# Experts: routing weights spread over partitions by DMA through device memory, shared expert as one block, rings of three

## The reference

```python
scores = sigmoid(x @ gate_w.T); choice = scores + e_bias        # 16 experts in 4 groups
# two best groups of four (by the sum of each group's best two), then the four best experts in them
topk_weight = scores[topk] / (sum + 1e-20) * 2.5
g = einsum('th,eih->eti', x, gate_proj); u = einsum('th,eih->eti', x, up_proj)   # 16 experts, 64 inner features
expert_out = einsum('eti,ehi->eth', silu(g) * u, down_proj)
y = einsum('tkh,tk->th', expert_out[topk_idx], topk_weight)
shared_out = silu(x @ shared_gate_w.T) * (x @ shared_up_w.T) @ shared_down_w.T
x = x + y + shared_out
```

## Time and profile before

| | us |
|---|---|
| median of 3 runs | 2615.48 (2614.51 to 2615.79) |
| the profiled execution, its own time | 2611.66 |
| its span, first to last instruction | 2609.8 |
| PE busy in the span | 2134.6 (82%) |
| DVE busy | 2013.6 (77%) |
| ACT busy | 1856.5 (71%) |
| POOL busy | 1645.0 (63%) |
| DMA, mean over the span | 6 GB/s |

### The profile page before, as it was taken

One profiled execution on the slowest core, in us unless ns is written; L12 is line 12 of the kernel. 1 busy time (PEld: TensorE's weight loads), 2 busy tenths in 40 slices (PEclk: granted clock), 3 DMA queues, 4 the chain that ended last, 5 costly groups with the idle time before them and its releaser, 6 DMA issues. The chain is left out here.

```text
span 2609.8 us, 51267 instructions
## 1 busy us (share of the span) xinstructions
PE 2134.6 (82%) x15144; PEld 1559.0 (60%) x15144; DVE 2013.6 (77%) x6071; ACT 1856.5 (71%) x3189; POOL 1645.0 (63%) x1508
## 2 busy tenths in 40 slices
PE   4999999999999789999966667666666776666599
PEld 3777777777777678888844444444444444433367
DVE  4777777777777666776658998999999899999522
ACT  2766666666676533334328999999999999999743
POOL 3667667777677200000028999999999999999600
PEclk7999999999999889999975666676776657767599
DMA  5000000000000000000000000000000000000011
GB/s 136 2 2 2 1 1 0 1 1 0 1 0 2 1 1 1 0 0 0 1 1 1 1 1 0 0 0 0 0 0 0 0 0 0 0 0 1 1 37 36
DMA packets 25280, 14.83 MB, mean 6 GB/s; under 512 B 2952, under 2 KB 24878, under 8 KB 25166
## 3 DMA queue, kind: packets, MB, share of 16 engines
q1 hardware_dynamic: 16846, 9.36, 1.3%
q10 hardware_dynamic: 8320, 4.19, 0.6%
HBM read 9.36 MB, written 4.19 MB: 5 GB/s over the span
## 5 line engine op out<-in xcount | busy, mean ns | idle before, releaser
L1445 POOL TENSOR_TENSOR u<-u,spare 128x1024 f32<-128x1024 f32 x256 | 597.1, 2375 | 41.6 <-ACT spare L1418 41.6
L553 ACT ACTIVATE prob<-s_ps,nmax 128x128 f32<-128x128 f32 (+1 forms) x1024 | 364.4, 432 | 140.2 <-DVE nmax L610 139.9
L1338 PE MATMUL d_ps<-rowsT 28*128 28x256 f32 x1024 | 171.7, 417 | 326.9 <-DVE u L1517 326.4
L610 DVE CUSTOM_DVE_ANT_0 s_ps<-s_ps,mask 128x128 f32<-128x128 f32 (+1 forms) x1024 | 340.7, 385 | 101.4 <-issue 78.0
L1338 PEld LDWEIGHTS d_ps<-rowsT 28*128 28x128 f32 x1024 | 111.6, 253 | 430.2 <-issue 429.5
L1513 DVE TENSOR_SCALAR u<-d_ps 128x1024 f32<-128x1024 f32 x256 | 311.9, 1218 | 41.7 <-PE i_ps L1338 41.1
L590 POOL TENSOR_TENSOR g_lo<-g_all,g_hi 128x512 fp32r<-128x512 f32 x256 | 329.0, 1285 | 21.4
L1517 DVE SCALAR_TENSOR_TENSOR u<-i_ps,u 128x1024 f32<-128x1024 f32 x256 | 313.5, 1225 | 14.8
L1456 POOL TENSOR_TENSOR spare<-spare,u 128x1024 f32<-128x1024 f32 x128 | 303.1, 2368 | 10.7
L1665 POOL MEMSET rows<- 128x4096 f32 x1 | 3.5, 3512 | 427.8 <-POOLq L352 427.8
L1432 ACT ACTIVATE u<-u 128x1024 f32<-128x1024 f32 x256 | 257.8, 1067 | 0.0
(11 more groups left out here) (267 smaller groups left out, 5699.6 us busy)
## 6 DMA issues: line engine op xcount, KB each, us to landing
x<-L_attn_x ACTq DMA_DIRECT2D x8, 512.0 KB, 13.8
y<-y_rows SPq DMA_DIRECT2D x16, 256.0 KB, 2.3
wkqv<-L_attn_Wkqv SPq DMA_DIRECT2D x4, 528.0 KB, 8.6
gate_rows<-L_ffn_gate_proj SPq DMA_DIRECT2D x1, 512.0 KB, 14.5
up_rows<-L_ffn_up_proj SPq DMA_DIRECT2D x1, 512.0 KB, 11.5
down_cols<-L_ffn_down_proj SPq DMA_DIRECT2D x1, 512.0 KB, 12.9
w<-L_ffn_w SPq DMA_DIRECT2D x2, 256.0 KB, 3.0
consts_sb<-consts SPq DMA_DIRECT2D x1, 256.0 KB, 4.4
```

The source lines that it names most:

```text
L553: last = nc.scalar.activation(prob[:, kind, at, :].rearrange("p c n -> p (c n)"), s_ps[kind][:, at.start * P:at.stop * P], ACT.Exp, bias=n ...
L610: last = nc.vector.tensor_tensor_reduce(out=scores, in0=scores, in1=keep.mask[:, N - width:N], scale=-1.0, scalar=3.4e38, op0=ALU.add, op1 ...
L1338: last = nc.tensor.matmul(ps[:, e * W2 + j * N:e * W2 + (j + 1) * N], rowsT[at, slot(i, p), 1, j * P:(j + 1) * P], rowsT[at, slot(i, p), 0 ...
L1445: nc.gpsimd.tensor_tensor(u[:, slot(i, p), :], u[:, slot(i, p), :], spare[:, p % SPARE, :], ALU.add).then_inc(sum_done, 1)
```

## The change

Four things change together in `moe`, and their preparation in `load_and_fold`:

1. The routing weights are no longer split into a high and a low part and spread by a matmul. They are turned (16 rows), copied to `wT`, written by a DMA to `w_rows` in device memory, read back by two DMAs that repeat each expert's row over 64 partitions, and land in `w_all`. VectorE's second product then reads `w_all` in place of `w_ps`.
2. The shared expert's gate and up weights stand side by side in one block of 128 columns, so that its slot has three matmuls instead of six.
3. `g_ps`, `u_ps`, `act_g` and `inter` have three buffers, and the down product follows two slots behind (`LAG`) instead of one.
4. The tables move: `WEIGHTS_AT` is (13, 14) for the two chunks of the next pair, and `ROUTE_AT` is 6 to 12 without a gap.

```diff
-    TAKEN = (0, 5, 11, 16, 17, 19, 23, 28)
+    TAKEN = (0, 5, 11, 16, 17, 19, 23, 26)
-    TURN_AT, LOGITS_AT, WEIGHTS_AT = (1, 3), (2, 4), 6
-    SCORE_AT, SPLIT_AT, ROUTE_AT = 5, (2, 14), (6, 7, 8, 10, 12, 13, 15)
+    TURN_AT, LOGITS_AT, WEIGHTS_AT = (1, 3), (2, 4), (13, 14)
+    SCORE_AT, SPLIT_AT, ROUTE_AT = 5, (2, 14), (6, 7, 8, 9, 10, 11, 12)
+    RING, LAG = 3, 2
...
-        wst = m.sb("wst", [P, T2, 2 * E], F32R)
-        wT = m.sb("wT", [P, 2, CHUNK], F32R)
+        weight = m.sb("weight", [P, T2, E])
+        wT = m.sb("wT", [E, 2, CHUNK])
+        w_all = m.sb("w_all", [P, 2, PAIRS, CHUNK])
+        w_rows = nc.dram_tensor("w_rows", [2, E, CHUNK], F32).ap()
...
                 after(dve, w_turned, 2 * r)
-                then(v.tensor_copy(wst[:, :, 0:E], rank[:, :, :]))
-                v.tensor_tensor(wst[:, :, E:2 * E], rank[:, :, :], wst[:, :, 0:E], ALU.subtract).then_inc(wst_done, 1)
+                v.scalar_tensor_tensor(out=weight[:, :, :], in0=test[:, :, :], scalar=SCALING,
+                                       in1=inv[:, :].unsqueeze(2).to_broadcast([P, T2, E]),
+                                       op0=ALU.mult, op1=ALU.mult).then_inc(wst_done, 1)
...
+                            if j < PAIRS:
+                                pe_split_product(nc, u_ps[q][:, :], keep.upT[0][:, j, :], keep.upT[1][:, j, :],
+                                                 x_hi[:, i, :], x_lo[:, i, :], True).then_inc(u_ready, 1)
                             pe_split_product(nc, g_ps[q][:, :], keep.gateT[0][:, j, :], keep.gateT[1][:, j, :],
                                              x_hi[:, i, :], x_lo[:, i, :], True).then_inc(g_ready, 1)
...
-                                nc.tensor.matmul(w_ps[q][:, :], keep.sel[:, j * P:(j + 1) * P], wT[:, i, :],
-                                                 start=True, stop=True).then_inc(w_ready, 1)
+                            if first and at == 1:
+                                pe_turn_weights(pe, 0, 0, 0, 2)
+                                pe_turn_weights(pe, 1, 1, 0, 2)
...
+            @block.sync
+            def _(sp):
+                def spread_weights(p, first):
+                    for i in range(2):
+                        c = 2 * p + i
+                        sp.wait_ge(wT_done, c + 1)
+                        sp.dma_start(w_rows[i], wT[:, i, :]).then_inc(w_written[i], 16)
+                        sp.wait_ge(w_written[i], 16 * (p + 1))
+                        if not first:
+                            sp.wait_ge(inter_done, (c - 1) * BLOCKS)
+                        for e in range(2):
+                            of_pairs = w_rows[i].rearrange("(j e) n -> e j n", e=2)[e]
+                            sp.dma_start(w_all[e * INTER:(e + 1) * INTER, i, :, :],
+                                         of_pairs.partition_broadcast(INTER)).then_inc(w_in[i], 16)
...
-                            dve.wait_ge(u_ready, n + 1)
-                            if not (early and j < 2):
-                                dve.wait_ge(down_done, n - 1)
...
+                                if j == 0:
+                                    dve.wait_ge(w_in[i], 32 * (p + 1))
+                                dve.wait_ge(gated_done, m2 + 1)
+                                if not (early and j < RING):
+                                    dve.wait_ge(down_done, n - RING + 1)
+                                nc.vector.tensor_tensor(inter[:, q, :], gated[:, j % 2, :], w_all[:, i, j, :],
                                                         ALU.mult).then_inc(inter_done, 1)
```

More of the change, by code:

```diff
@@ L40 @@
 WB = WIDTH // P
-PARTS = 3
 BIG = 1e15
@@ L153, in load_and_fold @@
                 transposes(ROUND, [rows[:, j, :] for j in range(j0, j0 + 4)], tuple(t[:, j0:j0 + 4, :] for t in pair))
-            transposes(ROUND, [rows[0:INTER, PAIRS, :]], tuple(t[:, PAIRS:PAIRS + 1, 0:INTER] for t in pair))
-        ups, downs = gates + 3, len(jobs)
+        ups, shared = gates + 2, len(jobs)
+        transposes(ROUND, [shared_rows[:, :]], tuple(t[:, PAIRS:PAIRS + 1, :] for t in keep.gateT))
+        downs = len(jobs)
         down = down_cols[:, 0:E, :].rearrange("p (j e) i -> p j (e i)", e=2)
@@ L244, in _ @@
                     elif n == ups:
+                        pe.wait_ge(up_in, 32)
+                    elif n == shared:
+                        pe.wait_ge(gate_in, 32)
                         pe.wait_ge(up_in, 32)
@@ L904, in pe_turn_x @@
             if i == 0:
-                after(pe, wT_done, c - 1)
+                after(pe, wT_done, c)
             else:
@@ L930, in pe_down @@
                 pe.wait_ge(res_done, c)
+            rows = P if j < PAIRS else INTER
             for t in range(TC):
-                last = nc.tensor.matmul(y_ps[:, t * P:(t + 1) * P], inter[:, q, t * P:(t + 1) * P],
-                                        keep.downT[:, j, :], start=(j == 0 and t == 0),
+                last = nc.tensor.matmul(y_ps[:, t * P:(t + 1) * P], inter[0:rows, q, t * P:(t + 1) * P],
+                                        keep.downT[0:rows, j, :], start=(j == 0 and t == 0),
                                         stop=(j == BLOCKS - 1), skip_group_check=True)
@@ L962, in act_wT @@
             act.wait_ge(w_turned, c + 1)
-            after(act, w_ready, (c - 1) * PAIRS)
-            nc.scalar.copy(wT[0:2 * E, i, :], misc[0:2 * E, :]).then_inc(wT_done, 1)
+            after(act, w_written[i], (c // 2) * 16 if isinstance(c, int) else (c - i) * 8)
+            nc.scalar.copy(wT[:, i, :], misc[0:E, :]).then_inc(wT_done, 1)
         def dve_route(dve, r, part):
@@ L1047, in dve_split_x @@
             dve.wait_ge(xTs_done, c + 1)
-            after(dve, u_ready, (c - 1) * BLOCKS)
+            after(dve, g_ready, (c - 1) * BLOCKS)
             nc.vector.tensor_copy(x_hi[:, i, :], xTs[:, i, :]).then_inc(x_rounded, 1)
@@ L1104, in body @@
                                 pe_logits(pe, 2 * p + 2 + LOGITS_AT.index(at), LOGITS_AT.index(at))
-                            if at == WEIGHTS_AT:
-                                pe_turn_weights(pe, c + 1, 1, p, 2 * p + 4 if ahead else chunks)
-                            if j > 0:
-                                pe_down(pe, n - 1, j - 1, 1 - q, c, early)
+                            if ahead and at in WEIGHTS_AT:
+                                pe_turn_weights(pe, 2 * p + 2 + WEIGHTS_AT.index(at), WEIGHTS_AT.index(at), p + 1, 2 * p + 4)
+                            if j >= LAG:
+                                pe_down(pe, n - LAG, j - LAG, (at - LAG) % RING, c, early)
                             elif not early:
-                                pe_down(pe, n - 1, BLOCKS - 1, 1 - q, c - 1, False)
-                    if ahead:
-                        pe_turn_weights(pe, 2 * p + 2, 0, p + 1, 2 * p + 4)
+                                pe_down(pe, n - LAG, BLOCKS + j - LAG, (at - LAG) % RING, c - 1, False)
                 over_pairs_ahead(pe, pairs, body)
-                pe_down(pe, chunks * BLOCKS - 1, BLOCKS - 1, 1, chunks - 1, False)
+                for j in range(BLOCKS - LAG, BLOCKS):
+                    pe_down(pe, (chunks - 1) * BLOCKS + j, j, (BLOCKS + j) % RING, chunks - 1, False)
             @block.scalar
@@ L1160, in _ @@
                 nc.gpsimd.memset(run[:, :].rearrange("p (t e) -> p t e", e=E)[:, :, 0:1], 0.0).then_inc(levels_set, 1)
+            @block.sync
[12 more added lines that the diff above has]
+                                         of_pairs.partition_broadcast(INTER)).then_inc(w_in[i], 16)
+                for p in range(pairs):
+                    spread_weights(p, p == 0)
             @block.vector
             def _(dve):
-                for at in range(2 * E, P, 2 * E):
-                    nc.vector.memset(wT[at:at + 2 * E, :, :].bitcast(F32), 0.0).then_inc(wT_cleared, 1)
                 dve_split_x(dve, 0, 0)
@@ L1191, in body @@
-                            if j == 4 and not early:
-                                dve.wait_ge(var_done, c * TC)
+                            if j == 3 and not early:
+                                dve.wait_ge(res_done, c)
+                            if j == 4 and not early:
+                                dve.wait_ge(stats_done, c * TC)
+                            if j == 5 and not early:
+                                dve.wait_ge(var_done, c * TC)
+                            dve.wait_ge(silu_done, n + 1)
@@ L1903, in first_block @@
         self.gateT = tuple(m.sb(f"gateT_{part}", [P, BLOCKS, P], F32R) for part in ("hi", "lo"))
-        self.upT = tuple(m.sb(f"upT_{part}", [P, BLOCKS, P], F32R) for part in ("hi", "lo"))
+        self.upT = tuple(m.sb(f"upT_{part}", [P, PAIRS, P], F32R) for part in ("hi", "lo"))
         self.downT = m.sb("downT", [P, BLOCKS, P])
@@ L1953, in constants @@
     c[0, C_LAST + P - 1] = 1
-    for part in range(PARTS):
-        for e in range(E):
-            c[part * E + e, C_SEL + e * INTER:C_SEL + (e + 1) * INTER] = 1
     return c
```

121 lines of the change are left out of this document (49 added, 72 removed).

## The result

The changed kernel takes 2625.58 us in the median of 5 runs (2620.34 to 2630.14), the kernel before 2615.17 beside it (5 runs, 2614.11 to 2615.79): a ratio of 1.0041, with an interval of 1.0025 to 1.0057. It is 0.4% slower. The profiled execution took 2620.34, its span is 2618.6, 8.8 longer than before. In the experiments further down nearly every kernel, the one before too, has executions of two lengths some 25 us apart (before: medians of 2613 and of 2636 to 2639), and the short ones are compared with short ones there, the long ones with long ones.

A forecast was written before the change was run, and what follows sets the result against it. TensorE was taken to bound the old expert stage, a chain through sigmoid, VectorE and turn the new (pair 49.5 against 50.8). Stage -6.8, preparation -0.67, DMA +2, clock +6: +0.5; 2611.7 + 0.5 + 3.8 = 2616 us, range 2597 to 2655.

The forecast's parts named there:

- likeliest case: Expert stage: the chains take the time summed for them, 2616 us, own range 2605 to 2628; chance 0.36.
- the waits in slots 11 and 13: Sign: TensorE waits about 3 us in each, released by VectorE's residual and by the routing weights.
- the sigmoid's starts: Sign: in the expert stage the router's sigmoid starts 49 to 50 us apart, once per pair of chunks.
- VectorE's slots 6 to 12: VectorE's part of the chain, from slot 6 until the next routing weights are ready: 19.6 us.
- the rival with a quicker VectorE: VectorE's second product takes 0.43 and gaps close: pair 46.4, total 2588, or 2565 if the chain gave way; chance 0.17.
- From the weights to the sigmoid: From T, when routing weights are ready, TensorE begins slot 5 at T + 24.1, VectorE slot 6 at T + 29.9.
- The DMA: Writing the turned weights and reading them back takes 10.2 to 13.0 us, 0.3 late in 7 pairs: 2 us.
- The rival of a late broadcast: Read-back at 170 GB/s: data take 12.3, 3.6 late in 7 pairs, 3.3 at the start, +28, 2644; chance 0.28.
- The start: First pair of the expert stage: weights land at 938.7, first down product at 939.9 where it was 931.10.
- The clock: TensorE's clock falls after its waits in the expert stage: 1.7 us in half the pairs, 7 x 0.85 = 6 us.
- The preparation: Before the expert stage, VectorE, which ends the preparation, has 0.67 us less to do.
- TensorE is the engine to follow: Reading of the old expert stage: TensorE busy 48.33 of 50 us at full clock, more than VectorE or ScalarE.

The follow-up runs named there:

- no_reread: Changed kernel with the two 1 MB broadcast reads issued only in the first pair of chunks, whose weights later pairs reuse; ratio 1.0031 to the kernel before.
- fill: Changed kernel with unread extra matmuls keeping TensorE busy in slots 11 and 13 of each pair but the last; ratio 1.0050 to the kernel before.
- shared_only: Kernel before with only the shared expert's gate and up made one block and a down product of 64 rows; ratio 0.9978 to the kernel before.
- no_table_before: Kernel before with silu in place of the router's sigmoid, so ScalarE loads no other table; ratio 0.9995 to the kernel before.
- late_pieces_res: Changed kernel with weight turns in slots 15 and 16, broadcast reads cut in two, residual ahead of VectorE's products in slots 1 and 10; ratio 0.9922 to the kernel before.

## Why the prediction came out as it did

I forecast 2616 and no change; it is 2625.6, slower by 0.4%. It lies in the likeliest case's own range (2605 to 2628), and half of my chances lay on slower. The mechanism of that case was right, a chain through VectorE in place of TensorE's own work; its terms were too small, by 7 us in all from the first down product to the last residual (389.7 as summed with DMA and clock, 396.6 measured): 5 of them in the six pairs from turn to turn (973.86 to 1282.77, 308.9), 3 in what follows, where 54.9 stand against some 52. Of its signs there were the waits in slots 11 and 13 (2.8 and 2.4), a clock below 1.00 and the reads landing after 10.1; the sigmoid's starts are 51.1 apart, not 49 to 50.

- **VectorE's slots 6 to 12**: 19.6 summed, 19.8 measured (1056.28 to the turn at 1076.05). The second product from SBUF takes 0.692, as taken; the rival with a quicker VectorE has nothing for it.
- **From the weights to the sigmoid** failed: T + 24.1 as summed, T + 24.65 in no_reread, where no broadcast is late, and slot 6 on VectorE at T + 30.6 in place of 29.9. (In the pair of the changed kernel shown above it is T + 25.0 and T + 30.9, the late broadcast in it.) The down product of the shared block, with 64 rows, takes 1.08 in place of 0.81 to 0.87 (last section), a slot with a router product is longer by 0.90 (I took 0.80), one with a turn by 0.44 (0.40). With 50.4 in no_reread against 49.5 the whole walk is 0.9 a pair too short, 5 in six: 0.55 here, 0.1 on ScalarE and 0.2 in VectorE's slots.
- **The DMA**: I took 0.3 late a pair; VectorE waits 1.8, and 0.5 reaches the period (50.9 in fill against 50.4 in no_reread, both at full clock). The chain from the write's issue took 14.0, where I had 10.2 to 13.0. The time allowed was as much too small: 17.1 less 2.7 is T + 14.4, not 14.0, and TensorE reached its down product of slot 20 at T + 17.85 (1093.80 in no_reread), not 17.1. That the two errors cancel, and 0.3 is nearly what one pair lost, is luck. Less the 1.5 of fixed time that I took, the 2.1 MB came in 10.9, 192 GB/s. That is near the figure of the Trainium skill, page "SBUF — State Buffer", section "Door 1: The DMA port swizzle" (196 GB/s for 1 MiB to 64 partitions); the trace agrees with it as far as the 1.5 holds, which no run measures, and I had left it out of the sum. The 12 to 14 us more that it gave there would have been too much, since 1.3 of each 1.8 is hidden.
- **The rival of a late broadcast** had this rate about right and its price wrong: it charged all of the lateness.
- **The start**: first down product 34.6 after the first turn, as summed 34.0 from the old start; the clock was low until 944. Right, with the weights there 1.0 later than summed and the down product sooner behind them.
- **The clock** was priced at 0.85 a pair and measured at 0.57 (51.47 in the changed kernel, 50.90 in fill). The sentence that "a low clock after the first wait is hidden by the second" failed all the same. Of the four stretches of low clock in these pairs one stands behind the turn, where I looked for it, and cost 1.6 (slot 18 begins 11.7 after the turn in place of 10.2); the other three stand behind the wait for the residual and cost 1.4, 0.5 and 0.6 (from slot 6 to the turn, against 19.8). In the pair after the one shown above (windows of 1 us, columns as above), that wait ends at 1119.5 and the clock is low up to 1126:

```profile
1118.00:1119.00 1.00, 0.00 (x0) 0.00 (x0) 0.93 (x2) 0.00 (x0) 0.00 (x0) 0.92 0.00 0
1119.00:1120.00 1.00, 0.49 (x2) 0.52 (x3) 0.96 (x4) 0.00 (x0) 0.00 (x0) 0.50 0.00 0
```

  and VectorE, in slot 12, waits for the silu of a product that TensorE made slowly:

```profile
1124.87 0.69 DVE L1201 TENSOR_TENSOR gated<-eu_ps,act_g 128x512 f32<-128x512 f32 x1 [1.65 <-ACT act_g L1138]
```

- **The preparation** was to end 0.67 sooner; the stage began 0.6 later. Not looked into.
- **"TensorE is the engine to follow"**, the reading that I began with, was half of it. TensorE was 97% busy, but a chain through the sigmoid and VectorE set the same 50.8: 0.9 us a pair off TensorE brought nothing (shared_only), 1.0 off the sigmoid 0.7 (no_table_before). The sum did not rest on it, but it would have told that the change takes load off one of two nearly equal limits, and lengthens the other.

So the expected gain went in this order: TensorE's 22 matmuls a pair (5.2 us) turned into waits for VectorE; the chain came to 50.4, not much under the old pair; lateness and clock took the rest, 0.5 and 0.6; and the first pair paid 9.4 for the longer way of its weights.

## What to carry to other kernels

An engine that is 97% busy need not be the only bound: walk the longest cycle of waits round once before taking work off it, for a second one may be as long. When results leave for device memory and come back, move their producer's hand-over off the loop's chain and split the transfer so that what is needed first comes first; here either edit alone gave 0.2 or lost 4.8 us a pair, and the two gave 3.4. Waits that stand in one chain trade places: price the cycle, never a single wait. And where a clock falls after waits, compare pairs at the same clock: by the means of its profile the cut broadcast saved 0.2 a pair, by the pieces of the cycle 0.5.

## What the runs showed of the hardware

- A down product with 64 rows is slower than one with 128. Eight of its matmuls, from their start to the next product's:

```profile
1047.94 1.16 PE L929 MATMUL y_ps<-downT,inter 64*128 64x128 f32 x8
1049.02 0.50 PE L61 MATMUL eu_ps<-x_hi,upT_hi 128*128 128x512 f32 x1
```

  1.08 in late_pieces_res, where the one with 128 rows at 1041.11 took 0.81 in the same profile. The cause is not settled.
- With the two reads under way the DMA share is 1.00 at 214 GB/s (window of the changed kernel, 932 to 936), where the load stage reached 341: a full share is no full rate.

```profile
932.00:936.00 4.00, 0.27 (x3) 0.17 (x2) 0.00 (x0) 0.32 (x2) 0.00 (x0) 0.81 1.00 214
```

- A write of 32 KB lands after 1.6 (median of 16, most with no reads ahead of them, no_reread) and after 5.7 in the median behind the reads of the chunk before: the next chunk's write seems to queue behind the reads.
